# The last gated network: TensorE's waits in a down round, and the round in which GpSimd makes the weight sums

## The chip, the cores and the metric

One core of a Trainium2 chip runs the whole program in one launch. The metric is the device time of that launch in microseconds (us). The kernel before took 3862.89 us (median of 3 runs, 3862.32 to 3865.49). Its profiled execution took 3863.55 us; the span from its first to its last instruction is 3861.7 us, and the granted TensorE clock over it is 0.966 of full speed on average.

## The reference, cut to what matters

The model has four layers, each a cross-attention block and a feed-forward block, on an input x of 4 x 512 x 512 in float32. The change is in the last feed-forward block:

```
def _L3_ffn_ref(x, w_gate, w_up, w_down):
    gate = jnp.einsum('bsd,hd->bsh', x, w_gate)
    up = jnp.einsum('bsd,hd->bsh', x, w_up)
    gated = jax.nn.silu(gate) * up
    return jnp.einsum('bsh,dh->bsd', gated, w_down)
...
x = x + jnp.tanh(g_ffn[3]) * _L3_ffn_ref(_layernorm(x, axis=-1), L3_ffn_w_gate, L3_ffn_w_up, L3_ffn_w_down)
```

The hidden size is 2048, the model size 512. Here is one batch row (512 tokens) after another; there are four.

## The kernel before

Each engine's instruction list is written out by hand, in program order, and the engines meet only through counting semaphores. `l3f_table` walks over the rounds once and numbers, for each engine, the jobs that it will finish (`F3[job]`): a wait on `made3` for `F3["H1", i - 1]` means that VectorE (DVE) has finished every job up to the second product of silu and up of round i - 1. `product3` counts TensorE's products, `taken3` ScalarE's jobs (ACT), `summed3` GpSimd's (POOL).

The block runs in 40 rounds (`ROUNDS3`). For each batch row there are four *up* rounds, one *down* round (output half 0), four more up rounds, and a down round (half 1): 32 up rounds and 8 down rounds. A round is one 2 x 2 block product by Winograd's scheme with seven products instead of eight, in the order `ORDER3 = (1, 2, 6, 5, 7, 3, 4)`. An up product is 4 matmuls, a down product 8, each of 128 x 128 weights on 256 columns in float32; TensorE runs each as two instructions, so that the trace shows 8 and 16. A product goes to the next of six PSUM banks in turn, and has to wait until the product six places before it has been taken out of that bank.

- **Weight sums.** Four of the seven left operands of an up round are sums of blocks of its weights (`S13`). GpSimd makes them with `up_term(u, k)`, k = 0 to 3 (L2962, L2964, L2966, L2968). Sum k may overwrite `S13` once the previous up round's product 5, 6, 7 or 3 has read it. Up round u has its sums made during up round u - 1: two before that round's own additions U4 (L2984) and C22 (L2986), two after them.
- **Taking out.** ScalarE copies products 1 and 5 out of PSUM (L2818) and applies silu (L2822). VectorE adds the others (L2889: C11, U2, U3, C12 and, in an up round, C21). GpSimd makes U4 from U3, and C22 from U4's operands.
- **Hidden tiles.** At an up round's end VectorE multiplies: H0 (L2906) writes `H3[0]` or `H3[1]`, H1 (L2908) writes `H3[2]` or `H3[3]`. Even rounds write tiles 0 and 2, odd rounds 1 and 3. After an odd round `hidden_terms` makes the down round's sums h0 to h3 (L2871 to L2876). In the first four up rounds VectorE also makes sums of the down weights, `w2_term` (L2866); after the last up round before a batch row ends, `x_terms` makes sums of the next input.
- **Down round on TensorE.** Product 1 multiplies `H3[0]`, product 2 `H3[1]`; products 6, 5, 7, 3 need the sums h0 to h3. `l3f_tensor` waits for H1 of the round before ahead of product 1, and for h3 ahead of product 6 (for the first down round also for the last `w2_term`).
- **Down round on VectorE.** It adds the scaled result to X (L2885: X11, X12, X22, X21a, X21). After half 0 of a batch row it goes on with the layer norm of the next one (`norm_vector`, L212 to L222), in which GpSimd makes one power (L228).

Weights of an up round come by DMA from SyncE (`l3f_sync`, L2706), three buffers deep; a buffer is free when its round's product 4 is done.

Of the kernel before, what the change touches and what calls it, by code (L numbers as in the profile page):

```python
# [92 lines left out]
def flamingo(nc, x, ctx_n, ctx_t, gates, gamma_raw, ident, l0_wq, l0_wk, hadamard, l0_w13, l0_w2, l1_wk, l1_bk, l1_bk_row,  # L93
# [3 lines left out]
    with ctx:  # L97
# [3 lines left out]
        def sem(name):  # L101
            return ctx.enter_context(nc.semaphore(name))
# [2512 lines left out]
        ROUNDS3 = []  # L2615
# [3 lines left out]
        UPS3 = [i for i, r in enumerate(ROUNDS3) if r[0] == "up"]  # L2619
# [13 lines left out]
        product3, taken3, made3, summed3 = sem("product3"), sem("taken3"), sem("made3"), sem("summed3")  # L2633

        def l3f_table():

            at, n = {}, {"pe": 0, "act": 0, "dve": 0, "pool": 0}

            def put(engine, *job):
                n[engine] += 1  # L2640
                at[job] = n[engine]
            for k in range(4):
                put("pool", "xt", 0, k)
            for k in range(4):
                put("pool", "w", 0, k)
            ups = pairs = 0
            for i, (kind, b, m) in enumerate(ROUNDS3):
                up = kind == "up"
                ups += up
                ahead = up and ups < len(UPS3)  # L2650
                for k in ORDER3:
                    put("pe", "p", i, k)
                for job in ("c1", "silu0", "c5", "silu1"):
                    if up or job[0] == "c":
                        put("act", job, i)
                for k in range(2 * ahead):
                    put("pool", "w", ups, k)
                put("pool", "U4", i)
                put("pool", "C22", i)
                for k in range(2, 4 * ahead):  # L2660
                    put("pool", "w", ups, k)
                put("dve", "C11", i)
                if up:
                    for job in ("U2", "U3", "C12", "C21", "H0", "H1"):
                        put("dve", job, i)
                    if m % 2:
                        for k in range(4):
                            put("dve", "h", pairs, k)
                        pairs += 1
                    if i < 4:  # L2670
                        put("dve", "w2", i)
                    if m == DUOS - 1 and b < B - 1:
                        for k in range(4):
                            put("dve", "xt", b + 1, k)
                else:
                    for job in ("X11", "U2", "U3", "C12", "X12", "X22", "X21a", "X21"):
                        put("dve", job, i)
            put("dve", "X21", i, 1)
            return at
        F3 = l3f_table()  # L2680
# [14 lines left out]
        def x_block(b, k, j):  # L2695
            return XT[:, b & 1, 2 * k:2 * k + 2, j * HALF_N:(j + 1) * HALF_N]

        def x_sum(b, k):
            return XT3[b & 1][:, k, :].rearrange("p (a n) -> p a n", a=2)
# [30 lines left out]
        def l3f_tensor(pe):  # L2730

            def up_operands(u, b):
                w = UP3[u % 3].rearrange("p k (u n) -> p k u n", u=2)
                sums = S13.rearrange("p k (u n) -> p k u n", u=2)
                left = {1: w[:, 0], 2: w[:, 2], 4: w[:, 3], 5: sums[:, 0], 6: sums[:, 1], 7: sums[:, 2], 3: sums[:, 3]}
                right = {1: x_block(b, 0, 0), 2: x_block(b, 1, 0), 3: x_block(b, 1, 1), 7: x_block(b, 0, 1),
                         5: x_sum(b, 0), 6: x_sum(b, 1), 4: x_sum(b, 2)}
                return left, right

            def up_product(k, bank, left, right):  # L2740
                for unit in range(2):
                    for kt in range(2):
                        last = nc.tensor.matmul(bank[:, unit * HALF_N:(unit + 1) * HALF_N], left[k][:, unit, kt * P:(kt + 1) * P], right[k][:, kt, :],  # L2743
                                                start=kt == 0, stop=kt == 1)
                return last

            def down_operands():
                left = {1: H3[0], 2: H3[1], 4: H3[3], 5: S23[0], 6: S23[1], 7: H3[2], 3: S23[2]}
                right = {1: W2B[0], 2: W2B[2], 3: W2B[3], 7: W2B[1], 5: W2T[0], 6: W2T[1], 4: W2T[2]}
                return left, right  # L2750

            def down_product(k, bank, left, right, half):
                n = DUOS // 2
                for row in range(2):
                    for unit in range(n):
                        last = nc.tensor.matmul(bank[:, row * HALF_N:(row + 1) * HALF_N], left[k][:, unit, row * P:(row + 1) * P], right[k][:, half * n + unit, :],
                                                start=unit == 0, stop=unit == n - 1)
                return last

            def turn_piece(kt):  # L2760
                if kt == 0:
                    pe.wait_ge(xn_ready, N_PE.step())
                bank = start_job(pe, turn, T_PE)
                for st in range(ST):
                    last = nc.tensor.transpose(bank[:, st * P:(st + 1) * P], XN[:, st, kt * P:(kt + 1) * P], ID[:, :])
                last.then_inc(turn.full, 1)

            ups = pairs = 0
            for i, (kind, b, n) in enumerate(ROUNDS3):
                up = kind == "up"  # L2770
                left, right = up_operands(ups, b) if up else down_operands()

                def product(k):
                    j = ORDER3.index(k)
                    if 7 * i + j >= len(BANKS3):
                        before = divmod(7 * i + j - len(BANKS3), 7)
                        pe.wait_ge(*emptied(before[0], ORDER3[before[1]]))
                    bank = bank3(i, k)
                    done = up_product(k, bank, left, right) if up else down_product(k, bank, left, right, n)
                    done.then_inc(product3, 1)  # L2780
                    if up and n == 6 and b < B - 1 and j < KT:
                        turn_piece(j)

                if up:
                    pe.wait_ge(up3_in[ups % 3], 16 * (ups // 3) + 16)
                    if n == 0 and b:
                        pe.wait_ge(turn.free, T_PE.now() + 2)
                else:
                    pe.wait_ge(w23_in, 64)
                    pe.wait_ge(made3, F3["H1", i - 1])  # L2790
                product(1)
                if i == 0:
                    pe.wait_ge(o_free, L3["out", NP3 - 1, 1, ST - 1] + 3)
                product(2)
                if up:
                    pe.wait_ge(summed3, F3["w", ups, 1])
                    if n == 0:
                        pe.wait_ge(made3 if b else summed3, F3["xt", b, 3])
                else:
                    pe.wait_ge(made3, F3["h", pairs - 1, 3])  # L2800
                    if i < 5:
                        pe.wait_ge(made3, F3["w2", 3])
                product(6)
                product(5)
                if up:
                    pe.wait_ge(summed3, F3["w", ups, 2])
                product(7)
                if up:
                    pe.wait_ge(summed3, F3["w", ups, 3])
                product(3)  # L2810
                product(4)
                ups, pairs = ups + up, pairs + (up and n % 2)
# [124 lines left out]
        def l3f_pool(pool):  # L2937
# [36 lines left out]
            ups = 0  # L2974
            for i, (kind, b, n) in enumerate(ROUNDS3):
                up, c = kind == "up", C3[i % 2]
                ups += up
                ahead = up and ups < len(UPS3)
                if ahead:
                    for k in range(2):  # L2980
                        up_term(ups, k)
                pool.wait_ge(taken3, F3["c5", i])
                pool.wait_ge(made3, F3["U3", i])
                tt(c[0], c[0], c[3], ALU.add).then_inc(summed3, 1)  # L2984
                pool.wait_ge(summed3, F3["U4", i])
                tt(c[3], c[3], c[2], ALU.add).then_inc(summed3, 1)  # L2986
                if ahead:
                    for k in range(2, 4):
                        up_term(ups, k)
                if kind == "down" and n == 0 and b < B - 1:  # L2990
                    norm_pool(pool)
# [176 lines left out]
```

## Time and profile before

| | |
|---|---|
| median of 3 runs | 3862.89 us |
| profiled execution, and its span | 3863.55 us, 3861.7 us |
| TensorE busy | 3591.1 us (93% of the span) |
| VectorE, ScalarE, GpSimd busy | 2169.4, 1407.1, 625.1 us |
| chain that ended last | TensorE 85%, VectorE 7%, issue 2%, GpSimd 2%, DMA 2%, ScalarE 2% |

The last gated network stands at the end of the program, from 3227.83 us on. In this stretch TensorE has a dense row of products; ScalarE, VectorE and GpSimd wait most of their time for them. "Issue" in the chain is time in which an engine stands still without a wait that the profile ascribes to another engine. The eight stretches of it in this network all stand at the beginning of a down round.

### The profile page before, as it was taken

The numbers are of one execution on the slowest core, as the hardware profiler recorded it, in microseconds if no ns is written. First come the engines' busy times: TensorE is split into PE (matmuls) and PEld (weight loads), VectorE is DVE, ScalarE is ACT, GpSimd is POOL, SyncE is SP. The second block draws the span as 40 slices with busy tenths as digits, with TensorE's granted clock in tenths as the row PEclk, the third lists the DMA queues.
The fourth block names the chain that finished last, engine by engine and source line by source line (L and its number), as shares of the span: only waits on it lengthen the run. The fifth ranks groups of instructions, "written<-read, shape, count | busy, mean of one in ns | idle before, by whom it ended". The sixth has DMA issues, their size and how long they took to land.

```text
span 3861.7 us, 38149 instructions
## 1 busy us (share of the span) xinstructions
PE 3591.1 (93%) x12973; PEld 1919.6 (50%) x12974; DVE 2169.4 (56%) x3831; ACT 1407.1 (36%) x2908; POOL 625.1 (16%) x588
## 2 busy tenths in 40 slices
PE   5999999996899998799769999999999998999999
PEld 2444444442455444466434444444444446888887
DVE  7656666136678876211147765666666665444544
ACT  7524252111367766222224343434344342111111
POOL 5100000000223331211110100000000004344443
PEclk8999999998899999899889999999999999999999
DMA  7321311310522232555621101010100003111210
GB/s 231 131 78 60 126 66 66 118 38 22 129 55 68 50 89 93 183 163 163 198 87 47 59 25 37 25 37 25 37 25 31 31 13 120 44 55 61 71 66 22
DMA packets 81846, 294.03 MB, mean 76 GB/s; under 512 B 17928, under 2 KB 18824, under 8 KB 66832
## 3 DMA queue, kind: packets, MB, share of 16 engines
q1 hardware_dynamic: 74304, 269.32, 21.4%
q0 software_dynamic: 7376, 22.57, 1.9%
q8 instruction: 96, 1.57, 0.2%
q14 instruction: 70, 0.57, 0.0%
HBM read 248.31 MB, written 38.81 MB: 74 GB/s over the span
## 4 chain that ended last, share of the span: by engine, by line
PE 85%; DVE 7%; issue 2%; POOL 2%; DMA 2%; ACT 2%; SPq 0%; DVEq 0%; ACTq 0%; POOLq 0%
PE BM L2315 6%; PE BM L2370 6%; PE BM L444 5%; PE BR L444 5%; PE BR L2381 4%; PE BS L2353 4%; PE BM L2743 3%; PE BR L2743 3%; PE BS L2743 3%; PE BS L460 3%; PE BT L2362 3%; PE BT L460 3%; PE BT L1589 3%; PE BM L2328 3%; PE BR L2021 3%; PE BM L2010 2%
## 5 line engine op out<-in xcount | busy, mean ns | idle before, releaser
L2446 ACT ACTIVATE AR<-BS,AR 128x512 f32<-128x512 f32 x256 | 174.6, 685 | 414.2 <-DVE AR L2538 414.2
L2551 DVE SCALAR_TENSOR_TENSOR X<-BR,AR,X 128x512 f32<-128x512 f32 x256 | 191.9, 750 | 206.0 <-PE BR L2381 196.6
L2538 DVE TENSOR_REDUCE AR<-BS 128x2 f32<-128x1024 f32 x128 | 157.0, 1226 | 251.0 <-PE BS L2353 251.0
L2440 ACT COPY AR<-BM 128x512 f32<-128x512 f32 x320 | 187.5, 586 | 263.7 <-PE BM L2370 100.1
L228 POOL TENSOR_TENSOR RSTD<-VAR,HALF 128x4 f32<-128x4 f32 x32 | 34.6, 1082 | 1464.3 <-DVE VAR L2567 930.5
L2381 PE MATMUL BR<-AR 128*128 128x512 f32 x512 | 254.6, 620 | 4.2 <-DVE X L2551 0.6
L2370 PE MATMUL BM<-AR 128*128 128x512 f32 x512 | 246.8, 594 | 0.0
L2315 PE MATMUL BM<-XT,AR 128*128 128x512 f32 x512 | 236.2, 605 | 0.7 <-ACT XT L241 0.7
L444 PE MATMUL BM<-XT,AR 128*128 128x512 f32 x512 | 231.7, 595 | 0.6 <-ACT AR L598 0.6
L444 PE MATMUL BR<-XT,AR 128*128 128x512 f32 x512 | 230.2, 592 | 0.0
L1681 ACT ACTIVATE PT<-BS 128x512 f32<-128x512 f32 x340 | 191.9, 596 | 73.3 <-PE BS L1579 68.2
L605 ACT ACTIVATE AR<-AR 128x512 f32<-128x512 f32 x256 | 182.5, 714 | 83.7 <-DVE AR L733 79.7
L2362 PEld LDWEIGHTS BT<-ID,AR 128*128 128x128 f32 x1024 | 128.2, 141 | 137.1 <-issue 125.6
L710 DVE TENSOR_SCALAR_CACHE_REDUCE AR<-AR 128x512 f32<-128x512 f32 x264 | 186.3, 743 | 3.5
L1743 DVE TENSOR_REDUCE NEG<-BM 128x2 f32<-128x1024 f32 x129 | 157.5, 1221 | 49.7 <-PE BM L1563 47.9
L2452 ACT COPY AR<-BT 128x512 f32<-128x512 f32 x256 | 151.5, 592 | 74.6 <-PE BT L2362 74.5
L1743 DVE TENSOR_REDUCE NEG<-BR 128x2 f32<-128x1024 f32 x127 | 155.0, 1220 | 30.4 <-PE BR L1563 27.9
L2381 PEld LDWEIGHTS BR<-AR 128*128 128x128 f32 x512 | 86.0, 189 | 170.7 <-DVE X L2551 88.9
L2315 PEld LDWEIGHTS BM<-XT,AR 128*128 128x128 f32 x512 | 92.2, 189 | 139.8 <-issue 116.2
L2353 PE MATMUL BS<-AR 64*128 64x512 f32 x512 | 147.4, 652 | 15.2 <-ACT AR L2446 14.5
L444 PEld LDWEIGHTS BM<-XT,AR 128*128 128x128 f32 x512 | 97.1, 191 | 124.2 <-issue 124.2
L444 PEld LDWEIGHTS BR<-XT,AR 128*128 128x128 f32 x512 | 97.3, 190 | 122.5 <-issue 122.5
(442 smaller groups left out, 6771.0 us busy)
## 6 DMA issues: line engine op xcount, KB each, us to landing
AR<-l_wq_dram SPq DMA_DIRECT2D x32, 1152.0 KB, 5.1
AR<-l_w_dram SPq DMA_DIRECT2D x36, 1024.0 KB, 4.8
AR<-l_w_dram SPq DMA_DIRECT2D x64, 512.0 KB, 3.2
AR<-l_w_dram SPq DMA_DIRECT2D x42, 768.0 KB, 4.9
AR<-w2h SPq DMA_DIRECT2D x16, 1024.0 KB, 4.8
QS<-qx SPq DMA_DIRECT2D x32, 512.0 KB, 9.6
AR<-l_w_dram SPq DMA_DIRECT2D x8, 1408.0 KB, 8.8
made<-AR SPq DMA_DIRECT2D x40, 256.0 KB, 4.8
```

What stands on the lines that cost most here:

```text
L444: last = nc.tensor.matmul(bank, w[:, kt, a, :], XT[:, b & 1, kt, :], start=kt == 0, stop=kt == KT - 1)
L460: last = nc.tensor.matmul(S_BANKS[st], f.HIDDEN[:, u, st * P:(st + 1) * P], f.DOWN[:, u, :], start=u == 0, stop=u == UG - 1)
L1681: nc.scalar.activation(PT2[:, tt, h, :], evict(("e", n, tt, h)), ACT.Exp, scale=float(HD ** -0.5)).then_inc(e_free, 1)
L1743: nc.vector.tensor_reduce(NEG2[:, n % 2, u // 2, to:to + 2], unit(("s", n, u))[:, 0:2, :], op=ALU.max, axis=AX.X, negate=True).then_inc(s_ ...
L2315: last = nc.tensor.matmul(bank, WS[:, p % 2, at:at + P], XT[:, b % 2, kt, :], start=kt == 0, stop=kt == KT - 1)
L2353: last = nc.tensor.matmul(BS[:, h, :], QRT[rows, st * P:(st + 1) * P], KRT[rows, :], start=True, stop=True)
L2362: last = nc.tensor.transpose(BT[:, L3[job] % 2, st * P:(st + 1) * P], PROB3[h][:, st, lt * P:(lt + 1) * P], ID[:, :])
L2370: last = nc.tensor.matmul(BM[:, L3[job] % 2, :], KVN[:, p // 8 * ST + lt, :], PROBT3[:, lt, :], start=lt == 0, stop=lt == ST - 1)
L2381: nc.tensor.matmul(BR[:, L3[job] % 2, :], CC3[h][:, st * P:(st + 1) * P], W3[:, p % 8 * 2 + h, :], start=True, stop=True)\
L2440: nc.scalar.copy(to, BM[:, L3[job] % 2, :]).then_inc(m_free, 1)
L2551: nc.vector.scalar_tensor_tensor(out=xb, in0=BR[:, L3[job] % 2, :], scalar=RS3[:, p % 2, h, st:st + 1], in1=xb, op0=ALU.mult, op1=ALU.add) ...
L2743: last = nc.tensor.matmul(bank[:, unit * HALF_N:(unit + 1) * HALF_N], left[k][:, unit, kt * P:(kt + 1) * P], right[k][:, kt, :], start=kt ...
```

## The change

Three lines. On TensorE a down round no longer waits for H1 of the round before ahead of product 1: it waits for H0 of the up round before that one (tile `H3[0]`), and, ahead of product 2, for H0 of the last up round (tile `H3[1]`). On GpSimd (and in the table of counts) the rule for the weight sums is now: a round makes the sums of the next up round if the round right after it is an up round. So the last up round before a down round makes none, and the down round makes those of the up round behind it.

```diff
             for i, (kind, b, m) in enumerate(ROUNDS3):
                 up = kind == "up"
                 ups += up
-                ahead = up and ups < len(UPS3)
+                ahead = ROUNDS3[i + 1:i + 2] and ROUNDS3[i + 1][0] == "up"
...
-                for k in range(2 * ahead):
+                for k in range(2 if ahead else 0):
                     put("pool", "w", ups, k)
                 put("pool", "U4", i)
                 put("pool", "C22", i)
-                for k in range(2, 4 * ahead):
+                for k in range(2, 4 if ahead else 2):
                     put("pool", "w", ups, k)
...
                 else:
                     pe.wait_ge(w23_in, 64)
-                    pe.wait_ge(made3, F3["H1", i - 1])
+                    pe.wait_ge(made3, F3["H0", i - 2])
                 product(1)
                 if i == 0:
                     pe.wait_ge(o_free, L3["out", NP3 - 1, 1, ST - 1] + 3)
+                if not up:
+                    pe.wait_ge(made3, F3["H0", i - 1])
                 product(2)
...
             for i, (kind, b, n) in enumerate(ROUNDS3):
                 up, c = kind == "up", C3[i % 2]
                 ups += up
-                ahead = up and ups < len(UPS3)
+                ahead = ROUNDS3[i + 1:i + 2] and ROUNDS3[i + 1][0] == "up"
                 if ahead:
                     for k in range(2):
                         up_term(ups, k)
```

GpSimd's instructions at the first down round, before. The first two rows are sums 0 and 1 of the fifth up round, then U4, C22 of the fourth, sums 2 and 3, then U4 and C22 of the down round, and the layer norm's power:

```order
L2962 TENSOR_TENSOR AR<-AR 128x512 [waits product3,up3_in1]
L2964 TENSOR_TENSOR AR<-AR 128x512 [waits product3,summed3]
L2984 TENSOR_TENSOR AR<-AR 128x512 [waits made3,taken3]
L2986 TENSOR_TENSOR AR<-AR 128x512 [waits summed3]
L2966 TENSOR_TENSOR AR<-AR 128x512 [waits product3,summed3]
L2968 TENSOR_TENSOR AR<-AR 128x512 [waits product3,summed3]
L2984 TENSOR_TENSOR AR<-AR 128x512 [waits made3,taken3]
L2986 TENSOR_TENSOR AR<-AR 128x512 [waits summed3]
L228 TENSOR_TENSOR RSTD<-VAR,HALF 128x4 [waits norm_var]
```

The same place now (every line number of this part is two higher: L2986 and L2988 are U4 and C22, L2964 to L2970 the sums):

```order
L2986 TENSOR_TENSOR AR<-AR 128x512 [waits made3,taken3]
L2988 TENSOR_TENSOR AR<-AR 128x512 [waits summed3]
L2964 TENSOR_TENSOR AR<-AR 128x512 [waits product3,up3_in1]
L2966 TENSOR_TENSOR AR<-AR 128x512 [waits product3,summed3]
L2986 TENSOR_TENSOR AR<-AR 128x512 [waits made3,taken3]
L2988 TENSOR_TENSOR AR<-AR 128x512 [waits summed3]
L2968 TENSOR_TENSOR AR<-AR 128x512 [waits product3,summed3]
L2970 TENSOR_TENSOR AR<-AR 128x512 [waits product3,summed3]
L228 TENSOR_TENSOR RSTD<-VAR,HALF 128x4 [waits norm_var]
```

Sums 0 and 1 have moved behind the up round's C22, sums 2 and 3 behind the down round's C22; the same holds at seven of the eight down rounds (behind the last there is no up round).

TensorE's first down round, from the last product of the up round to product 5; these rows are the same in both kernels, and only the counts for which the two waits of products 1 and 2 on `made3` stand differ:

```order
L2743 MATMUL BR<-AR 128x256 [waits taken3]
L2743 MATMUL BR<-AR 128x256 x3
L2756 MATMUL BS<-AR 128x256 [waits made3,w23_in]
L2756 MATMUL BS<-AR 128x256 x7
L2756 MATMUL BS<-AR 128x256 [waits made3]
L2756 MATMUL BS<-AR 128x256 x7
L2756 MATMUL BM<-AR 128x256 [waits taken3,made3]
L2756 MATMUL BM<-AR 128x256 x7
L2756 MATMUL BM<-AR 128x256 [waits made3]
```

No instruction was added or moved on TensorE.

## Rows read from the trace of the kernel before

**Rows 1.** The page: busy time of each engine, share of the span.
```profile
PE 3591.1 (93%) x12973; PEld 1919.6 (50%) x12974; DVE 2169.4 (56%) x3831; ACT 1407.1 (36%) x2908; POOL 625.1 (16%) x588
```

**Rows 2.** Chain that ended last, second down round: start, us, engine, bank, line.
```profile
3356.30 3.71 issue
3360.01 6.35 PE BR L2756 x16
3366.36 6.91 PE BS L2756 x32
...
3387.08 3.45 PE BS L2743 x16
```

**Rows 3.** Groups by line from 3240 us, down products: busy, mean ns | idle before.
```profile
L2756 PE MATMUL BS<-AR 128*128 128x256 f32 x304 | 72.1, 397 | 11.1 <-issue 11.1
L2756 PE MATMUL BR<-AR 128*128 128x256 f32 x304 | 72.0, 397 | 9.7 <-issue 9.7
L2756 PE MATMUL BM<-AR 128*128 128x256 f32 x288 | 67.3, 393 | 7.4 <-issue 7.4
```

**Rows 4.** Stretches of the eight down rounds: length, busy by engine, PEclk, DMA.
```profile
3276.34:3306.14 29.80, 26.09 (x113) 22.77 (x114) 13.75 (x16) 1.37 (x3) 5.51 (x5) 0.94 0.10 36
...
3829.18:3855.87 26.69, 24.42 (x113) 21.20 (x112) 10.15 (x15) 1.31 (x3) 2.65 (x3) 1.00 0.04 14
sum 235.66, PE 207.46 PEld 180.56 DVE 100.63 ACT 10.91 POOL 41.23; mean PE 25.93 PEld 22.57 DVE 12.58 ACT 1.36 POOL 5.15
```

**Rows 5.** Timeline into the second down round: start, us, engine, line [idle before].
```profile
3355.20 1.27 POOL L2986 TENSOR_TENSOR AR<-AR 128x512 f32<-128x512 f32 x1
...
3356.43 1.27 POOL L2966 TENSOR_TENSOR AR<-AR 128x512 f32<-128x512 f32 x1
...
3357.23 1.02 DVE L2906 TENSOR_TENSOR AR<-AR 128x512 f32<-128x512 f32 x1
3357.78 1.59 POOL L2968 TENSOR_TENSOR AR<-AR 128x512 f32<-128x512 f32 x1
3358.17 1.74 DVE L2908 TENSOR_TENSOR AR<-AR 128x512 f32<-128x512 f32 x1
...
3360.01 6.35 PE L2756 MATMUL BR<-AR 128*128 128x256 f32 x16 [3.71 <-issue]
...
3361.88 0.68 DVE L2876 TENSOR_TENSOR AR<-AR 128x512 f32<-128x512 f32 x1
```

**Rows 6.** Timeline, first down round: the last sum of down weights.
```profile
3282.52 2.29 DVE L2866 TENSOR_TENSOR AR<-AR 128x2048 f32<-128x2048 f32 x1
```

**Rows 7.** Timeline into the last down round, where GpSimd makes no sums.
```profile
3830.66 0.68 DVE L2908 TENSOR_TENSOR AR<-AR 128x512 f32<-128x512 f32 x1
...
3831.44 3.69 PE L2756 MATMUL BR<-AR 128*128 128x256 f32 x16 [2.26 <-issue]
```

**Rows 8.** Stretches behind two of the gaps, and between two: columns as Rows 4.
```profile
3360.01:3366.36 6.35, 6.35 (x17) 5.12 (x18) 5.02 (x8) 0.00 (x0) 0.00 (x0) 0.58 0.08 34
...
3756.43:3763.57 7.14, 7.14 (x33) 6.31 (x34) 2.52 (x4) 0.59 (x1) 0.00 (x0) 1.00 0.06 25
...
3306.14:3356.30 50.16, 50.16 (x241) 43.69 (x239) 28.92 (x43) 11.25 (x20) 29.53 (x23) 1.00 0.18 64
```

**Rows 9.** Timeline behind the first down round, and one GpSimd sum before it.
```profile
3259.22 2.56 POOL L2962 TENSOR_TENSOR AR<-AR 128x512 f32<-128x512 f32 x1 [3.98 <-PE BS L2743]
...
3301.52 1.26 POOL L2986 TENSOR_TENSOR AR<-AR 128x512 f32<-128x512 f32 x1
...
3303.52 2.08 DVE L2885 SCALAR_TENSOR_TENSOR X<-AR,G,X 128x512 f32<-128x512 f32 x3
...
3313.08 1.28 DVE L2889 TENSOR_TENSOR AR<-AR,BM 128x512 f32<-128x512 f32 x2
...
3318.07 3.62 PE L2743 MATMUL BM<-XT,AR 128*128 128x256 f32 x16
```

## The prediction, made before the changed kernel ran

> **What bounds the kernel now.** I read the page first. TensorE is busy for 93% of the span [rows 1], so a change gains only where TensorE stands still or runs slowly. Next I read the chain that ended last, over the last network. It is TensorE's row of products, broken only at the start of each down round: a stretch of "issue" and then products that take too long. In the second down round TensorE stands for 3.71 us, its first product takes 6.35 us, and from then on two products take 6.91 us, so 3.45 each [rows 2]. The groups by line give the whole of the standing: 11.1 + 9.7 + 7.4 = 28.2 us ahead of the eight down rounds [rows 3].
>
> What ends it is read from the timeline, since "issue" names nobody. VectorE's second multiplication H1 ends at 3358.17 + 1.74 = 3359.91, and TensorE starts at 3360.01 [rows 5]. In the last down round H1 ends at 3830.66 + 0.68 = 3831.34 and TensorE starts at 3831.44 [rows 7]. So the gap is the wait for H1 on product 1, and a signal takes 0.10 us to be acted on. H1 is long where GpSimd sums weights beside it (1.74 us against 0.68, with H0 at 1.02), which is why the last gap is 2.26 and not 3.71 us.
>
> The second loss is speed. Behind the gap of the second round the granted clock is 0.58 of full speed over 6.35 us, a mixture of the two levels 1.2 and 2.4 GHz; in the 50 us of unbroken products between two down rounds it is 1.00 [rows 8]. Before the fall TensorE had stood still. Behind the gap of the seventh round the clock stays at 1.00, and its first two products take 7.14 instead of 6.91 us [rows 8]: 0.23 us is what merely starting again costs.
>
> **The change, part by part.** First the size of what can go. Six products at full speed take 3387.08 - 3366.36 = 20.72 us [rows 2], so a down round without a gap takes 20.72 x 7/6 = 24.17 us. The eight take 235.66 us together, from 29.80 for the first to 26.69 for the last [rows 4]. The excess is 235.66 - 8 x 24.17 = 42.3 us: 28.2 of standing, 8 x 0.23 = 1.8 of starting, and the remaining 12.3 of slow clock.
>
> *Product 1* now waits for the H0 of the up round before the last, which ended about 10 us before: H0 follows its round's end by 2 us (3358.25 against 3356.30), and an up round is 7 products of 1.73 us (two in 3.45 [rows 2]), 12.1 us. Its bank was emptied in the last up round. So it starts when the last up product ends, at 3356.30 in the second round, and covers 3.45 us.
>
> *Product 2* waits for the last round's H0, which ends at 3357.23 + 1.02 = 3358.25 [rows 5]; product 1 ends at 3356.30 + 3.45 = 3359.75. This wait has 1.4 us in hand after the signal's 0.10, so it costs nothing while product 1 runs.
>
> *Product 6* is what comes late next. It waits for h3, which ends at 3361.88 + 0.68 = 3362.56 [rows 5], 3362.66 with the signal. TensorE arrives at 3356.30 + 6.91 = 3363.21. That is 0.55 us in hand: little, but nothing to pay, if VectorE's chain does not get longer. It should not, because GpSimd works at the same place as before: C22 starts at 3355.20, sums 2 and 3 at 3356.43 and 3357.78 [rows 5]. In their place now stand sums 0 and 1, of the same shape, whose waits (last round's products 5 and 6, weights loaded rounds before) are met. So I do not count the 1.4 us that H0 and H1 would save without company. Sums 0 and 1 no longer stand ahead of U4, so the chain behind U4 can come sooner but not later; I put this at nothing.
>
> *The first down round* is different: product 6 there also needs the last sum of the down weights, which VectorE runs behind h3. It ends at 3282.52 + 2.29 = 3284.81 [rows 6], with the signal 3284.91. The round begins at 3276.34 [rows 4], so TensorE arrives at 3283.25. A gap of 1.66 us stays, and 0.23 for starting: 1.9 us. Whether the clock falls behind it is open: from nothing (as behind the last round's 2.26 us, whose product takes 3.69 [rows 7]) up to 6.35 - 3.45 = 2.9 us [rows 2]. I take nothing, the row of the nearest gap.
>
> *Sums 2 and 3* move to the end of the down round, behind its C22. In the first round that ends at 3301.52 + 1.26 = 3302.78 [rows 9]; two sums of 1.27 (at most 2.56, the longest in these rows) end by 3305.4 to 3308. The next up round needs them for its products 7 and 3, four products of 1.73 after its start at 3306.14, so at 3313. At least 5 us in hand. GpSimd's next job, the layer norm's power, needs X21 and VectorE's statistics, which follow the round's last product at 3306.14, and so isn't held up. No DMA and nothing in SyncE's queue moves, and the weight buffers are freed by products whose order is unchanged.
>
> There they run beside VectorE's X12, X22 and X21a, three operations in 2.08 us [rows 9], which so far had no company. The price has to be bounded: nothing, or for three operations the 1.74 - 0.68 = 1.06 us that H1 lost, 3.2 us. Behind them come X21, the norm, and C11 of the next up round, done at about 3313.08 + 0.69 = 3313.77; TensorE needs its bank for the first product of the round after, at 3318.07 [rows 9]. That is 4.3 us in hand, so even 3.2 us stay off the path. I take nothing.
>
> **The sum.** 42.3 - 1.9 = 40.4 us less. The profiled execution took 3863.55 us (span 3861.7), which becomes 3823.1. It is 0.66 us above the median of the runs, 3862.89; against that median the forecast is 3822.5.
>
> **The rivals.**
> *A, product 6 takes the place of product 1.* If sums 0 and 1 hold H0 and H1 up a little more than sums 2 and 3 did, the 0.55 us are gone. For it: the smallest reserve of the change, at all rounds alike. Against: same shapes, same place. With a GpSimd sum at 2.56 instead of 1.59, h3 is 0.97 later, TensorE waits 0.42 and starts again for 0.23: 0.65 x 7 = 4.6 us, so 3827.
>
> *B, the clock falls for another reason.* If standing still isn't what lowers it, only standing and starting go: 28.2 + 1.8 - 1.9 = 28.1 us, 3835. For it: behind the gap of the seventh round there was no fall, so one doesn't follow from the other every time. Against: the fall shown stands right behind a gap, and the unbroken 50 us ahead of it show none [rows 8].
>
> *C, the additions to X wait for whole sums.* X12, X22 and X21a each stand still while a moved sum runs, and with them X21, the norm, C11 and the bank that the second up round's first product needs. Two sums of 1.27 us are 2.5 us, inside the 4.3 in hand; two of 2.56 are 5.1, so 0.8 us too late at each of the three down rounds with a norm behind them: 2.4 us, so 3825. For it: H0 and H1 with and without company [rows 5, 7]. Against: the long sum is the rare one. The Trainium skill has this as a rule ("SBUF — State Buffer", "Who interferes with whom"): a VectorE operation with two inputs in SBUF and a GpSimd operation that reads SBUF exclude each other for a whole instruction, and the later one waits; H0's 1.02 and H1's 1.74 us agree with it, and it speaks against this part of the change.
>
> *D, slower.* The same place, but without measure: C11 late by far more than 4.3 us behind each down round with a norm, TensorE then standing there for the excess. To use up 40.4 us at three places it takes 4.3 + 13.5 = 17.8 us of delay at each, and from there the time is 3863.5 less the usual 0.66, 3863, or more. Against it: the three additions and two sums at their longest come to 2.1 + 5.1 us.
>
> *E, no change.* Product 1 is held by something else as well, at the same time as H1, say the bank or the weights: 3863. Against: the gap's end follows H1 by 0.10 us both where H1 takes 1.74 and where it takes 0.68.
>
> **How the numbers follow.** Forecast 0.71, A 0.12, B 0.07, C 0.05, D 0.02, E 0.03. The forecast's own range is 3820.5 (nothing stays in the first round either) to 3825.5 (a clock fall of 2.9 us there). To leave out no more than 2 in 10 I take A in and a little beyond: 3819.5 to 3829. A measurement tells this kernel from no change at about 0.2%, 7.7 us. The forecast, A, B and C all lie beyond that: faster 0.95; E: same 0.03; D: slower 0.02.
>
> **What would show it.** In the profile after, the chain has no "issue" ahead of product 1; the eight down rounds take about 24.2 us each, the first 26; the clock over them is 1.00; H0 and H1 still take about 1.0 and 1.7 us except before the last. A gap ahead of a product 6 in the second round shows A. Clocks under 0.9 without a gap show B. A gap ahead of the first product of a second up round shows C or, if long, D. I am wrong if the eight rounds together do not fall to about 195 us, or if the up rounds get longer by more than 2 us in all.

## The result and the profile after

The changed kernel takes 3820.66 us (median of 4 runs, 3820.28 to 3823.32), the kernel before 3863.05 us (median of 4, the three shown and one beside the changed kernel). The ratio is 0.9891, 95% interval 0.9874 to 0.9908: 42.4 us faster. The forecast was 3822.5 us, range 3819.5 to 3829.

The page of the changed kernel's profiled execution (3820.56 us, span 3818.7), busy time by engine, answers to [rows 1]: TensorE's share rises, although its busy time falls by 16 us; 13.9 of these lie in the down rounds, where products ran slowly (207.46 us of busy PE [rows 4], 193.60 below).

```profile
PE 3575.0 (94%) x12973; PEld 1910.2 (50%) x12974; DVE 2180.0 (57%) x3831; ACT 1406.0 (37%) x2908; POOL 627.4 (16%) x588
```

The eight down rounds of the changed kernel as stretches (length, busy time of PE, PEld, DVE, ACT, POOL, granted clock, DMA share, GB/s), which answer to [rows 4]:

```profile
3273.80:3299.81 26.01, 24.41 (x113) 21.19 (x113) 14.20 (x15) 1.30 (x3) 8.27 (x7) 1.00 0.12 41
3349.97:3374.14 24.17, 24.17 (x113) 21.28 (x113) 14.50 (x18) 1.30 (x3) 8.29 (x7) 1.00 0.13 44
...
3788.70:3812.89 24.19, 24.18 (x113) 20.93 (x111) 10.14 (x15) 1.31 (x3) 2.64 (x3) 1.00 0.04 15
sum 195.22, PE 193.60 PEld 169.78 DVE 104.13 ACT 10.42 POOL 60.62; mean PE 24.20 PEld 21.22 DVE 13.02 ACT 1.30 POOL 7.58
```

They fell from 235.66 to 195.22 us, by 40.4. Seven are as long as seven products at full speed, the clock is 1.00 in all, and the first holds 1.84 us more.

The chain that ended last, of the changed kernel (start, us, what), at the network's first products, the first and second down round and the end; the second part answers to [rows 2]:

```profile
3225.44 3.45 PE BM L2743 x16
...
3280.00 2.21 DVE AR L2868
3282.21 0.09 issue
3282.30 7.14 PE BM L2756 x32
...
3349.97 3.45 PE BR L2756 x16
3353.42 6.91 PE BS L2756 x32
...
3805.97 6.92 PE BR L2756 x32
```

The 3.71 us of issue and the first product of 6.35 us are gone. One break is left: in the first down round the chain goes over VectorE's last sum of down weights (L2868), and product 6 starts behind it at 3282.30.

The ends of the same chain in the kernel before:

```profile
3227.99 3.45 PE BM L2743 x16
...
3848.95 6.92 PE BR L2756 x32
```

So the network, from its first product to the end of its last, took 3848.95 + 6.92 - 3227.99 = 627.88 us and takes 3805.97 + 6.92 - 3225.44 = 587.45. That is the 40.4 us of the sum. The other 2.55 us between the two profiled executions lie ahead of the network, where no instruction was changed.

### The profile page after: what moved, and what is told of

The parts are those of the page before. It is cut to its first block, busy times and chain, and to the rows that moved or that the text cites. A ratio compares the mean times of both kernels' runs of the same rounds, so it can differ in the third digit from the quotient of the medians.

```text
span 3818.7 us, 38157 instructions
## 1 busy us (share of the span) xinstructions
PE 3575.0 (94%) x12973; PEld 1910.2 (50%) x12974; DVE 2180.0 (57%) x3831; ACT 1406.0 (37%) x2908; POOL 627.4 (16%) x588
## 4 chain that ended last, share of the span: by engine, by line
PE 85%; DVE 8%; POOL 2%; DMA 2%; ACT 2%; issue 1%; SPq 0%; DVEq 0%; ACTq 0%; POOLq 0%
PE BM L2315 6%; PE BM L2370 6%; PE BM L444 5%; PE BR L444 5%; PE BR L2381 4%; PE BS L2353 4%; PE BM L2743 3%; PE BR L2743 3%; PE BS L2743 3%; PE BS L460 3%; PE BT L2362 3%; PE BT L460 3%; PE BT L1589 3%; PE BM L2328 3%; PE BR L2021 3%; PE BM L2010 2%
```

## The experiments

All times of a network below are counted in this way, from the chain of each run's profile; "before" beside a median is the kernel before, run on the same chip in the same rounds. Each network time is that of the one profiled execution of its run. Of each edit the engine's own lines are shown, with "..." for lines left out; where an edit moves jobs of GpSimd or VectorE, `l3f_table` gets the same order, which is not shown.

**The changed kernel again (label again), no edit.**

> The changed kernel once more, as the reference of this series. It took 3820.7 us, 2 us less than the sum of the prediction gives; in the two traces the network itself is 627.88 and 587.45 us long, from its first product to the end of its last, which is the predicted 40.4 us, and the other 2.5 us lie before the network. If those are chance (the clock's falls come at other moments in each execution), the stretch before the network differs by up to 3 us from run to run and the network again takes 587.5 us. If they belong to the change, the network begins at about 3225.4 us every time.

3823.41 us against 3861.38, ratio 0.9898 (0.9882 to 0.9915). The network starts at 3228.13 us and takes 587.49. In the eleven profiles of this study it starts between 3225.44 and 3231.90 us. So the 2.55 us were chance, and only the network's own length compares kernels that differ by 1 or 2 us.

**Only TensorE's waits (label waits_only).**

```diff
--- before
+++ waits_only
-                    pe.wait_ge(made3, F3["H1", i - 1])
+                    pe.wait_ge(made3, F3["H0", i - 2])
                 product(1)
...
+                if not up:
+                    pe.wait_ge(made3, F3["H0", i - 1])
                 product(2)
```

> Only TensorE's waits are changed, GpSimd makes the weight sums where it did before. Theory, the waits carry the whole gain: sums 2 and 3 stand beside H0 and H1 for as long as sums 0 and 1 do in the changed kernel, so product 6 keeps about 0.5 us in hand; no gap but the 1.6 us of the first down round; 3820.7 us, within 1. Rival, the move of the sums is needed: product 6 comes late at seven down rounds by about 0.4 us and starts again for 0.23, 3825 us.

3821.67 us against 3861.38, ratio 0.9897 (0.988 to 0.9913); network 587.56 us, 0.1 more than with both edits. The groups by line of this run (busy, mean ns | idle before), down products and additions to X:

```profile
L2756 PE MATMUL BS<-AR 128*128 128x256 f32 x304 | 67.4, 379 | 0.0
L2756 PE MATMUL BR<-AR 128*128 128x256 f32 x304 | 67.4, 379 | 0.0
L2756 PE MATMUL BM<-AR 128*128 128x256 f32 x288 | 63.9, 379 | 1.7 <-DVE AR L2868 1.7
...
L2887 DVE SCALAR_TENSOR_TENSOR X<-AR,G,X 128x512 f32<-128x512 f32 x32 | 22.6, 749 | 0.6
```

The only idle time ahead of a down product is the 1.7 us of the first round, and the additions to X keep their 0.75 us (1.03 in the changed kernel, where sums stand beside them). The waits carry the whole gain; the rival is out.

**Only GpSimd's sums (label sums_only).**

```diff
--- after
+++ sums_only
-                    pe.wait_ge(made3, F3["H0", i - 2])
+                    pe.wait_ge(made3, F3["H1", i - 1])
                 product(1)
...
-                if not up:
-                    pe.wait_ge(made3, F3["H0", i - 1])
                 product(2)
```

> Only GpSimd's sums are moved, TensorE waits for H1 ahead of product 1 as before. Theory: the moved sums 0 and 1 stand at the same place beside H0 and H1, so the gaps stay at 3.6 to 3.7 us and the clock falls behind most of them: 3863 us, no change. Rival, the move frees H0 and H1 from company: gaps of 2.3 us at all eight and fewer falls, 3840 to 3853 us.

3860.43 us (median of 10) against 3862.23, ratio 0.9997 (0.9987 to 1.0007): no change. From its chain, the first and the third down round:

```profile
3276.17 3.64 issue
3279.82 8.81 PE BS L2756 x32
...
3435.13 3.64 issue
3438.77 7.14 PE BR L2756 x32
```

The gap is 3.64 instead of 3.71 us: 0.07 is all that GpSimd's move does for U4. The rival's gaps of 2.3 us did not come, except at the last round, which had one before. In the profiled execution the network takes 624.17 us, 3.7 less than before, of which 0.5 is the gaps; the rest is the clock, which here fell behind four gaps and before behind six.

**Product 1 waits for half of it (label half_wait).**

```diff
--- after
+++ half_wait
-                    pe.wait_ge(made3, F3["H0", i - 2])
+                    pe.wait_ge(made3, F3["H0", i - 1])
                 product(1)
```

> The changed kernel, but product 1 too waits for H0 of the last up round, not only product 2. Theory: a gap of 3358.25 + 0.10 - 3356.30 = 2.05 us at seven down rounds and 1.7 at the last, 16 us, plus 8 x 0.23 for starting, less the 1.8 of the first round whose sum now is in time: 3836.7 us if no clock falls, up to 3849 if the clock falls as it did behind 3.71 us (12.3 us over all). If standing lowers the clock, the falls are fewer than behind 3.71 us. Rival B, the clock falls for another reason: as many falls as before, 3849 us, or none at all.

3841.56 us against 3862.23, ratio 0.9947 (0.9931 to 0.9964); network 606.43 us, 19.0 more than in the changed kernel. Chain, the second and the sixth down round:

```profile
3352.17 1.97 issue
3354.14 5.38 PE BR L2756 x16
...
3658.14 1.97 issue
3660.11 3.69 PE BS L2756 x16
```

The sum closes: seven gaps of 1.98 and one of 1.65 are 15.5 us, less the 1.6 of the first round that is now covered; seven more starts of 0.23 are 1.6; and two rounds, the second and fourth, with a first product of 5.38 instead of 3.69 us are 3.4. Together 18.9. The clock over these two products is 0.68, over the six others 1.00. Gaps of 2 us lower it in two cases of seven, those of 3.7 us in six of seven before. These are single executions, so the counts alone are thin. What puts rival B out is the chain of all eleven profiles: each of the thirteen falls in the network stands right behind a gap of 1.97 us or more, and in the seven profiles without a gap over 1.7 us no product of the network ran slowly (clock 1.00). So the falls go with standing, but a gap of a given length does not settle whether there is one; what does stays open.

**h3 later by two additions (label late_h3).**

```diff
--- after
+++ late_h3
                 v.wait_ge(made3, F3["h", pair, 1])
+                if q:
+                    for k in (1, 2):
+                        tt(c[k], at(H3[1]), at(S23[1]), ALU.subtract)
                 tt(at(S23[2]), at(H3[1]), at(S23[1]), ALU.subtract).then_inc(made3, 1)
```

> The changed kernel with two more additions of 128 x 512 on VectorE (into tiles that nobody reads) ahead of h3 at each down round: h3 comes 1.2 us later. Theory, product 6 has 0.6 us in hand: it waits 0.6 us and starts again for 0.23 at six down rounds, 1.2 us more in the first, nothing at the last: 5 + 1.2 = 6.2 us, 3827 us; more by 1.9 to 2.9 us wherever the clock falls. Rival, another wait stands behind product 6 and the reserve is larger: no gap, 3821 to 3822 us.

3831.2 us against 3862.23, ratio 0.992 (0.9903 to 0.9936); network 595.28 us, 7.8 more than in the changed kernel. Timeline at the second down round: the two additions, h3, and product 6:

```profile
3364.83 1.29 DVE L2880 TENSOR_TENSOR AR<-AR 128x512 f32<-128x512 f32 x2
3366.03 0.68 DVE L2881 TENSOR_TENSOR AR<-AR 128x512 f32<-128x512 f32 x1
...
3366.77 3.50 PE L2756 MATMUL BS<-AR 128*128 128x256 f32 x15 [0.56 <-DVE AR L2881]
```

h3 came 1.2 us later and product 6 waited 0.56, at each of six rounds: 0.6 us were in hand, as the prediction had it (0.55). The first round's gap grew to 2.8 us, and there the clock fell (8.83 instead of 7.14 us for two products), which is the 1.7 us over the expected 6.2. The median is 4.2 us over its expectation of 3827; the rest of that lies outside the network or is scatter between executions.

**All sums behind C22 (label sums_late).**

```diff
--- after
+++ sums_late
+                first = (2 if up else 0)
                 if ahead:
-                    for k in range(2):
+                    for k in range(first):
                         up_term(ups, k)
...
                 if ahead:
-                    for k in range(2, 4):
+                    for k in range(first, 4):
                         up_term(ups, k)
```

> The changed kernel, but in a down round all four weight sums stand behind C22. Theory: H0 and H1 stand alone, the first gap falls from 1.6 to 0.2 us; X12, X22 and X21a have company from two more sums but only three operations to be held up, so X21 and C11 come no later than in the changed kernel, where C11 behind a norm still has 2.7 us in hand: 3819.3 us. Rival C, the longer row of sums delays X21, the norm and C11 by 2 to 3 us more: gaps of up to 1 us at three second up rounds, 3820 to 3823 us.

3821.61 us against 3862.23, ratio 0.99 (0.9884 to 0.9917); network 586.10 us, 1.35 less than in the changed kernel, as expected. But my reason was half wrong. Timeline behind the first down round: the additions to X, the norm's last step, C11, and the product that needs C11's bank:

```profile
3298.17 4.40 DVE L2888 SCALAR_TENSOR_TENSOR X<-AR,G,X 128x512 f32<-128x512 f32 x3
...
3307.61 3.82 DVE L222 TENSOR_SCALAR XN<-X,MV,RSTD 128x512 f32<-128x512 f32 x4 [1.13 <-POOL RSTD L228]
...
3311.35 1.27 DVE L2892 TENSOR_TENSOR AR<-AR,BM 128x512 f32<-128x512 f32 x2
...
3312.72 3.62 PE L2744 MATMUL BM<-XT,AR 128*128 128x256 f32 x16
```

I had expected no delay beyond that of the changed kernel. C11 ends at 3312.04 and its bank is needed at 3312.72: 0.7 us in hand, where the changed kernel has 2.7 and the one before 4.3. Rival C's delay is real, and here it nearly reaches the path.

**Sums in the middle of the down round (label sums_in_mid).**

```diff
--- after
+++ sums_in_mid
+                first = (2 if up else 4)
                 if ahead:
-                    for k in range(2):
+                    if not up:
+                        pool.wait_ge(made3, F3["C11", i])
+                    for k in range(first):
                         up_term(ups, k)
...
                 if ahead:
-                    for k in range(2, 4):
+                    for k in range(first, 4):
                         up_term(ups, k)
```

> The changed kernel, but in a down round GpSimd begins all four weight sums once VectorE has made C11, when the hidden sums are done, and ends them before U4. Theory: H0 and H1 fall to 0.69 us each there, h3 comes 1.4 us sooner; only the first down round was late, so its gap falls from 1.6 to 0.2 us and nothing else changes: 1.4 us less, 3819.3 us; X12, X22 and X21a go back to 2.08 us. Rival, GpSimd's time beside C11 to U2 costs: a gap in a down round or a late U4, 3821 us or more.

3821.19 us against 3861.38, ratio 0.9893 (0.9876 to 0.9909); network 586.05 us, 1.4 less than in the changed kernel. Timeline, first down round: H0 and H1 without company, and product 6:

```profile
3277.50 0.69 DVE L2909 TENSOR_TENSOR AR<-AR 128x512 f32<-128x512 f32 x1
3278.11 0.68 DVE L2911 TENSOR_TENSOR AR<-AR 128x512 f32<-128x512 f32 x1
...
3283.76 7.14 PE L2757 MATMUL BM<-AR 128*128 128x256 f32 x32 [0.21 <-DVE AR L2869]
```

The gap is 0.21 us instead of 1.60. X12, X22 and X21a are back at 2.08 us, as expected; X11, which I had left out, now has company (1.86 us) and costs nothing. The rival's gap did not come.

**And the last sum of down weights behind round 2 (label sums_and_w2).**

```diff
--- sums_in_mid
+++ sums_and_w2
-                    if i < 4:
-                        w2_term(i)
+                    for k in ((0,), (1,), (2, 3))[i] if i < 3 else ():
+                        w2_term(k)
```

> As the one with the sums in the middle of the down round, and the last sum of the down weights is made behind round 2 instead of round 3. Theory: what is left of the gap at the first down round is that sum of 2.28 us behind h3; with it gone no gap is left in the network, which takes 587.5 - 1.8 = 585.6 us; 3818.8 us. Rival, 4.6 us of weight sums behind round 2 make VectorE late for the banks of round 3: a gap of 1 to 2 us there, 3820 us.

3819.97 us against 3861.38, ratio 0.9892 (0.9875 to 0.9908); network 585.98 us, only 0.07 less than without it. Timeline at the first down round, its products 1 and 2, and H0:

```profile
3274.47 7.39 PE L2757 MATMUL BS<-AR 128*128 128x256 f32 x32
...
3277.39 0.69 DVE L2909 TENSOR_TENSOR AR<-AR 128x512 f32<-128x512 f32 x1
```

And product 2 in the chain of this run:

```profile
3278.13 3.72 PE BS L2757 x16
```

The gap ahead of product 6 is gone, but the two products take 7.39 instead of the 7.07 us that they take on this view in sums_in_mid. H0 ends at 3278.08, just when product 1 does; product 2 starts 0.05 us later by the chain and takes 3.72 instead of 3.45 us, which is the cost of starting again. Two sums of down weights behind round 2 had made VectorE late all through round 3. The rival had the lateness, but neither theory had product 2 as the place.

**The version that follows (label no_gap).** The same with `((0, 1), (2,), (3,))[i]`: two sums of down weights behind round 0.

> Weight sums in the middle of the down round, and the sums of the down weights made two behind round 0, one behind round 1, one behind round 2, none behind round 3. Theory: behind round 2 no longer 4.6 but 2.3 us of them stand, so H0 of round 3 comes in time for product 2, which it missed by 0.05 us with two there (and 0.23 us for starting again); no gap over 0.03 us is left in the network, which takes 587.6 - 1.6 - 0.23 = 585.8 us, 1.8 less than in the changed kernel. Median 3817 to 3822 us, by where the clock falls before the network. Rival: two sums behind round 0 make VectorE late for round 1, and a gap of 0.1 to 2 us comes back there.

3819.69 us against 3862.19, ratio 0.989 (0.9874 to 0.9907). Chain at the first down round, and its ends:

```profile
3226.26 3.45 PE BM L2744 x16
...
3271.16 3.45 PE BR L2744 x16
3274.61 6.91 PE BS L2757 x32
3281.52 6.91 PE BM L2757 x32
...
3804.97 6.92 PE BR L2757 x32
```

The network takes 585.63 us, 1.82 less than in the changed kernel, and TensorE's products follow each other without a break. (The expectation counts from the first matmul itself, 0.15 us earlier.) On the medians, which chance moves by a few us ahead of the network, this kernel can't be told from the changed one.

## Why the prediction was right

- *Product 1 and the gap.* Right in place and size: 28.2 us of standing went, and only the first round kept 1.60 (forecast 1.66). The waits alone give it (waits_only); half of the wait brings half of the gaps back (half_wait).
- *The slow clock.* Right: 12.3 us went with the gaps; 1.00 in all eight rounds now. The 12.3 was a remainder, but the chain of the kernel before gives it directly: its six falls cost 1.69, 2.66, 1.69, 1.64, 1.69 and 2.80 us beyond starting, 12.2 in all. Which gap lowers the clock is not predictable from its length (half_wait, sums_only). That gaps make a kernel's runs spread more is not shown: the ten runs of sums_only lie between 3857.39 and 3866.45 us, but the thirteen of the kernel before beside them, with as many gaps, between 3860.24 and 3863.85.
- *The clock behind the gap that stays.* Taken as nothing from one row, with up to 2.9 us left open, and it came so, behind this gap in all three profiles that have it (1.60, 1.62 and 1.68 us; changed kernel, again, waits_only). There is some luck in this: gaps of 1.98 us lowered the clock in two cases of seven.
- *Starting again, 0.23 us.* Right: 7.14 against 6.91 us behind the gap that is left; 0.26 to 0.27 in late_h3 and sums_and_w2.
- *Product 6 has 0.55 us in hand.* Right, and shown from the other side by late_h3. The reason was right too: sums 0 and 1 hold H0 and H1 up just as sums 2 and 3 had done. Timeline of the changed kernel into the second down round (GpSimd's sums 0 and 1, H0, H1, h3), which answers to [rows 5]:

```profile
3350.03 1.27 POOL L2964 TENSOR_TENSOR AR<-AR 128x512 f32<-128x512 f32 x1
...
3350.82 1.02 DVE L2908 TENSOR_TENSOR AR<-AR 128x512 f32<-128x512 f32 x1
3351.38 1.60 POOL L2966 TENSOR_TENSOR AR<-AR 128x512 f32<-128x512 f32 x1
3351.77 1.75 DVE L2910 TENSOR_TENSOR AR<-AR 128x512 f32<-128x512 f32 x1
...
3355.49 0.68 DVE L2878 TENSOR_TENSOR AR<-AR 128x512 f32<-128x512 f32 x1
```

h3 ends at 3356.17, with the signal 3356.27; product 6 is due at 3353.42 + 3.45 = 3356.87. So GpSimd's half of the change does nothing for the time, and waits_only and sums_only confirm it.

- *Sums 2 and 3 beside the additions to X.* I took nothing from a range of 0 to 3.2 us of delay. The delay is there and stays off the path. Timeline of the changed kernel behind the first down round, which answers to [rows 9]:

```profile
3297.18 3.38 DVE L2887 SCALAR_TENSOR_TENSOR X<-AR,G,X 128x512 f32<-128x512 f32 x3
3297.75 1.59 POOL L2970 TENSOR_TENSOR AR<-AR 128x512 f32<-128x512 f32 x1
...
3305.59 2.87 DVE L222 TENSOR_SCALAR XN<-X,MV,RSTD 128x512 f32<-128x512 f32 x4 [1.13 <-POOL RSTD L228]
...
3308.38 1.27 DVE L2891 TENSOR_TENSOR AR<-AR,BM 128x512 f32<-128x512 f32 x2
...
3311.73 3.62 PE L2743 MATMUL BM<-XT,AR 128*128 128x256 f32 x16
```

The norm's last step in the kernel before, where no sum ran beside it:

```profile
3311.25 1.92 DVE L222 TENSOR_SCALAR XN<-X,MV,RSTD 128x512 f32<-128x512 f32 x4 [1.13 <-POOL RSTD L228]
```

The three additions take 3.38 instead of 2.08 us, and C11 ends 2.7 us ahead of its bank's next product instead of 4.3. The prediction priced only the additions. Behind them VectorE used to wait 0.65 us for the round's last product, so of the 1.30 us that they lost only about half reaches X21 and the norm (0.67 us later, counted from the round's end); the larger part of C11's delay, 0.95 us, is the norm's last step (2.87 instead of 1.92), which now runs beside the next sums and for which the prediction had no term. The additions have two inputs in SBUF, and the trace agrees with the rule of the Trainium skill named in rival C ("SBUF — State Buffer", "Who interferes with whom") as far as they slow beside GpSimd's sums; that they stand still for whole sums is not shown, since they lost 1.30 us and not the 2.5 of two sums. The price on the path was nothing.

- *The sum.* 40.4 us forecast, 40.43 measured in the network. The median came out 1.8 us below the forecast. The stretch ahead of the network takes 3225 to 3232 us by chance, and in the profiled execution 2.55 us of the gain lie there; the step that turned its time into a median had no term for that. That the median is low for the same reason is likely but not shown, since the other runs left no trace. Of the rivals, A (no gap in the second round), B, D (2.7 us still in hand) and E (product 1 starts without a gap) are out; C's mechanism is there in part, its price is not.

## What to carry to other kernels

Let a product wait for the tile that it reads, not for the last job of the round before; first find the wait that comes late next, and how much it has in hand, because that says whether the whole gap goes. Moving another engine's work away from the critical stretch gains nothing if work of the same length moves into its place: here sums 0 and 1 replaced sums 2 and 3 (nothing), and only with no sum there did the first down round gain 1.4 us (sums_late, sums_in_mid). Two kernels that differ by a thousandth are better compared by the length of the stretch that was changed than by the whole time.

## What the runs showed of the hardware that I had not expected

- A gap of the same length does not always lower TensorE's clock: it fell behind 6 of 7 gaps of 3.7 us before, 4 of 7 of 3.64 us (sums_only), 2 of 7 of 1.98 us (half_wait), once behind 2.8 us (late_h3), and never behind those of 0.56 and 1.6 to 1.7 us, nor behind the 2.26 us of the last down round (before, sums_only). A fall cost 1.6 to 2.9 us beyond starting. Each count is from one profiled execution, and what decides a case is open.
- A wait that is late by 0.05 us costs 0.3 us of TensorE's time, since starting again costs 0.23 to 0.27 whether the wait was 0.05 (sums_and_w2), 0.56 (late_h3) or 3.70 us (before, seventh round).
- The norm's last step (L222, one tensor input and two scalars) also slows beside GpSimd's sums: four take 2.87 us in the changed kernel and 3.82 in sums_late; before and in sums_in_mid, where it ended ahead of the sums, the four took 1.92. The Trainium skill ("SBUF — State Buffer", "Who interferes with whom") lists this kind of operation among those that can take the port shared with GpSimd, if its operands meet certain conditions; the slowing agrees with that, but no run here tests the conditions.
